# A decoder layer in fp32 quality on one core: batch 1's queries multiplied from raw weights beside batch 0's, and another order of cutting the weights

## What is computed

```
x = layernorm(x + attention(x))        # 16 heads of 64, rope on q and k, causal, w_q w_k w_v w_out
x = layernorm(x + conv(x, context))    # 3 taps, weighed with cosines of neighbouring context columns
x = layernorm(x + ffn(x))              # activations in 8 bits, ternary weights, silu(gate) * up, down
```

## Time and profile before

| | us |
|---|---|
| median of 3 runs | 1465.19 (1463.82 to 1466.19) |
| profiled execution: time, span | 1463.32, 1461.4 |
| set-up, up to the last raw product | 73.2 of the span |
| turn 0 | 73.2 to 142.44 |
| turn 1 | 142.44 to 192.11 |
| PE busy over the span | 1382.8 (95%) |
| DVE, ACT, POOL busy | 1068.1, 613.3, 231.6 |

### The profile page before, as it was taken

One profiled execution on the slowest core, in us unless ns is written; L12 is line 12 of the kernel. 1 busy time (PEld: TensorE's weight loads), 2 busy tenths in 40 slices (PEclk: granted clock), 3 DMA queues, 4 the chain that ended last, 5 costly groups with the idle time before them and its releaser, 6 DMA issues.

```text
span 1461.4 us, 23278 instructions
## 1 busy us (share of the span) xinstructions
PE 1382.8 (95%) x7576; PEld 695.5 (48%) x7576; DVE 1068.1 (73%) x1846; ACT 613.3 (42%) x1203; POOL 231.6 (16%) x270
## 2 busy tenths in 40 slices
PE   6787999999989999999999969999999999999996
PEld 2343555555545555554554544444444444444443
DVE  2886554555477787777877577888888888888884
ACT  4765654555455455445545342222222222222221
POOL 0112121212112221321322311000000000000000
PEclk9898999999999999999999979999999999999999
DMA  9502635454434534444443177222222222222200
GB/s 367 211 14 103 208 128 176 130 191 140 157 118 140 176 117 163 144 143 157 141 172 116 49 250 180 85 74 72 75 83 72 72 72 72 72 72 72 72 19 24
DMA packets 63570, 178.91 MB, mean 122 GB/s; under 512 B 15360, under 2 KB 26672, under 8 KB 63536
## 3 DMA queue, kind: packets, MB, share of 16 engines
q1 hardware_dynamic: 63536, 178.48, 37.5%
HBM read 153.02 MB, written 25.43 MB: 122 GB/s over the span
## 4 chain that ended last, share of the span: by engine, by line
PE 44%; issue 42%; DVE 5%; POOL 3%; ACT 2%; DMA 2%; SPq 1%; POOLq 0%; ACTq 0%; DVEq 0%
PE ps L484 36%; PE ps L475 3%; PE ps L576 2%; PE ps L558 2%; DMA ctx<-ctx 1%; POOL q L1324 1%; ACT tern L831 1%; DVE weights L1024 1%; PE ps L533 1%; ACT prob L753 1%; POOL rstd L1319 1%; DVE weights L1023 1%; DVE negmax L1058 0%; DVE prob L1069 0%; SPq L363 0%
## 5 line engine op out<-in xcount | busy, mean ns | idle before, releaser
L484 PE MATMUL ps<-weights,xT 128*128 128x512 f16 x2160 | 484.6, 381 | 0.0
L484 PEld LDWEIGHTS ps<-weights,xT 128*128 128x128 f16 x2160 | 209.7, 98 | 242.4 <-issue 9.8
L629 PE MATMUL ps<-weights 128*128 128x512 fp8e4 (+1 forms) x1536 | 300.0, 357 | 0.9 <-issue 0.9
L629 PEld LDWEIGHTS ps<-weights 128*128 128x128 bf16 x1536 | 146.7, 98 | 156.0 <-issue 1.4
L484 PE MATMUL ps<-weights 128*128 128x512 f16 x768 | 171.6, 384 | 7.6 <-issue 6.2
L851 ACT ACTIVATE weights<-ps,xscale 128x512 f32<-128x512 f32 x96 | 61.7, 643 | 249.2 <-PE ps L629 249.2
L655 PE MATMUL ps<-weights 128*128 128x512 fp8e4 x704 | 157.3, 380 | 0.0
L753 ACT ACTIVATE prob<-prob,negmax,undo 128x128 f32<-128x128 f32 x256 | 122.7, 482 | 20.7 <-DVE negmax L1060 20.7
L484 PEld LDWEIGHTS ps<-weights 128*128 128x128 f16 x768 | 75.7, 99 | 100.5 <-issue 10.7
L655 PEld LDWEIGHTS ps<-weights 128*128 128x128 bf16 x704 | 67.7, 98 | 76.0 <-issue 0.5
L1319 POOL TENSOR_TENSOR rstd<-rstd,expo 128x1 f32<-128x1 f32 x32 | 17.3, 541 | 535.9 <-DVE rstd L953 535.9
(11 more groups left out here) (145 smaller groups left out, 1836.9 us busy)
## 6 DMA issues: line engine op xcount, KB each, us to landing
wch<-w_ffn SPq DMA_DIRECT2D x96, 688.0 KB, 4.3
wch<-sim_scratch SPq DMA_DIRECT2D x96, 128.0 KB
ternary_scratch<-tern SPq DMA_DIRECT2D x48, 172.0 KB, 1.9
ctx<-ctx SPq DMA_DIRECT2D x16, 512.0 KB
weights<-x SPq DMA_DIRECT2D x16, 512.0 KB, 10.5
x_scratch<-weights SPq DMA_DIRECT2D x16, 512.0 KB, 2.9
weights<-x_scratch SPq DMA_DIRECT2D x16, 512.0 KB, 3.3
out<-k SPq DMA_DIRECT2D x16, 512.0 KB, 2.7
```

Of the source, the lines that this page charges most:

```text
L484: ins = nc.tensor.matmul(ps[:, bank], partsT[:, a, t], weights[:, t, w, half * HALF:(half + 1) * HALF], start=(t == 0 and a + w == 0), sto ...
L629: ins = nc.tensor.matmul(ps[:, 2 * w + a, 0:n], xqT[:, t], w8m[:, t, at:at + n], start=(t == 0), stop=(t == KT - 1))
```

## The change

Batch 1's queries (j = 0 and 2) are multiplied in `first_qkv(0)` too, in fp32 from the same raw tiles of w_q, into the two banks `OB` that the attention's output uses later; `proj(0)` and `proj(2)` of turn 0 fall away. The input of batch 1 is loaded right after that of batch 0 and ahead of all weights. ACT squares w_q and w_k without a break, then makes batch 1's high part, squares w_v, makes the high parts of w_k, squares w_o. The four norms come earlier on PE and alternate between banks 4 and 5. ACT makes the high parts of tiles 8 to 15 and 20 to 31. Turn 0 has an order of its own on PE, ACT, DVE and POOL: all eight absolute sums stand at its end on ACT, the context's sums behind the cuts on DVE. Later turns are as before (their code moves into `turn_rest`, not shown). The diff, cut to its core; the two waits added in `scores` and `pv` hold back writes to banks 4, 6 and 7 until `w_factors(3)` and the ropes of batch 1's queries have read them.

```diff
-SPLITS_ACT = [n for n in range(4 * KT) if n % 4 and not 2 * KT <= n < 3 * KT]
...
-                if t == KT - 1:
+                if t == KT - 1 and m == 0:
+                    eng.wait_ge(q1_full, 2)
+                elif t == KT - 1:
                     eng.wait_ge(pj_full[1], m + 1)
                 else:
                     eng.wait_ge(raw_used, (KT - 1) * m + t + 1)
...
-        NORM = 7
+        NORM = 4
...
                     sp.dma_start(weights[:, n + 2:n + 4] if n < 4 * KT - 2 else wo_raw[:], w.rearrange("(k p) n -> p k n", p=P)[:, 2 * h:2 * h + 2]) \
                         .then_inc(w_in[m][h], 16)
-                if m == 0:
-                    sp.dma_start(x_in[:], xT_in[1]).then_inc(x_loaded, 16)
...
                 if has_next2:
                     sp.wait_ge(parts_ready, b + 2)
+                    if isinstance(b, int) and b == 0:
+                        sp.wait_ge(q1_full, 2)
...
                 m, half = ((0, 0), (1, 0), (0, 1), (1, 1), (2, 0), (2, 1))[j]
-                if j == 0:
+                if isinstance(n, int) and n == 1:
+                    if j in (0, 2):
+                        return
+                    pe.wait_ge(parts_ready, 2)
+                    pe.wait_ge(w_split, (m + 1) * KT)
+                elif j == 0:
...
                 pe.wait_ge(w_squared, KT * (m + 1))
-                nc.tensor.matmul(ps[:, NORM, KT * m:KT * (m + 1)], ones, wsq[:, m], start=True, stop=True) \
-                    .then_inc(w_norm, 1)
+                if m >= 2:
+                    pe.wait_ge(w_norm_sum, m - 1)
+                nc.tensor.matmul(ps[:, NORM + m % 2, 0:KT], ones, wsq[:, m], start=True, stop=True).then_inc(w_norm, 1)
...
                 at = (PJ, TR, PJ)[m]
+                if m == 0:
+                    pe.wait_ge(x_loaded, 16)
...
                         pe.wait_ge(w_in[m][t // 2], 16)
-                    for half in range(2):
-                        ins = nc.tensor.matmul(ps[:, at + half], v[:, t * P:(t + 1) * P],
-                                               weights[:, KT * m + t + 2, half * HALF:(half + 1) * HALF],
-                                               start=(t == 0), stop=(t == KT - 1))
-                        if t == KT - 1:
-                            ins.then_inc(pj_full[half], 1)
+                    for xb, bank in ((v, at), (x_in, OB)) if m == 0 else ((v, at),):
+                        for half in range(2):
+                            ins = nc.tensor.matmul(ps[:, bank + half], xb[:, t * P:(t + 1) * P],
+                                                   weights[:, KT * m + t + 2, half * HALF:(half + 1) * HALF],
+                                                   start=(t == 0), stop=(t == KT - 1))
+                            if t == KT - 1 and bank == OB:
+                                ins.then_inc(q1_full, 1)
+                            elif t == KT - 1:
+                                ins.then_inc(pj_full[half], 3 if m == 2 and half == 0 else 1)
                     if t < KT - 1:
                         ins.then_inc(raw_used, 1)
-                    if t == (KT - 1, KT - 2, KT - 3)[m]:
-                        w_total(m)
...
+                    if isinstance(b, int) and b == 0:
+                        pe.wait_ge(w_norm_sum, 4)
...
+                    if isinstance(b, int) and b == 0:
+                        pe.wait_ge(q1_free, u + 1)
...
+                if isinstance(b, int) and b == 0:
+                    qk_T(0)
+                    proj(1)
+                    scores(0)
+                    qk_T(1)
+                    proj(3)
+                    scores(1)
+                    prob_T(0)
+                    proj(4)
+                    pv(0)
+                    prob_T(1)
+                    pv(1)
+                    proj(5)
+                    for c in range(2):
+                        pe.wait_ge(pj_free[c], pj_out(b))
+                        pe.wait_ge(oT_ready, b * 2 + 2)
+                        product(PJ + c, oT, w_parts[:, 3], c, 3 * KT if c == 0 else None).then_inc(pj_full[c], 1)
+                    return
...
+                def turn_first():
+                    for w in range(2):
+                        copy_bank(w, tr_pair(0, 0), qkT[:, w])
+                    for n in range(2 * KT + 5, 3 * KT):
+                        high_w(n)
+                    act.wait_ge(scores_full, 1)
+                    for w in range(2):
+                        copy_bank(w, tr_pair(0, 1), qkT[:, w])
+                    exps(0)
+                    high_w(3 * KT)
+                    high_w(3 * KT + 1)
+                    for w in range(2):
+                        copy_bank(w, tr_pair(0, 2), probT[:, w])
+                    exps(1)
+                    high_w(3 * KT + 2)
+                    high_w(3 * KT + 3)
+                    oT_high_part(0)
+                    act.wait_ge(pv_full, 1)
+                    for w in range(2):
+                        copy_bank(w, tr_pair(0, 3), probT[:, w])
+                    high_w(3 * KT + 4)
+                    oT_high_part(1)
+                    v_chunk(1, 0)
+                    for n in range(3 * KT + 5, 4 * KT):
+                        high_w(n)
+                    act.wait_ge(ctx_loaded, 32)
+                    nc.scalar.square(sq[:], ctx9[:]).then_inc(ctx_squared, 1)
+                    abs_chunk(0)
+                    v_chunk(1, 1)
+                    abs_chunk(1)
+                    high_x(2)
+                    for c in range(2, SUMS):
+                        abs_chunk(c)
+                if first:
+                    turn_first()
+                    return
...
-            for n in range(KT):
+            for n in range(2 * KT):
                 square(n)
-                if n == 1:
-                    high_x(1)
-            for n in range(2 * KT):
-                square(n + KT)
-                if n in SPLITS_ACT:
-                    high_w(n)
+            high_x(1)
+            for n in range(2 * KT, 3 * KT):
+                square(n)
+            for n in range(KT, 2 * KT):
+                high_w(n)
+            for n in range(3 * KT, 4 * KT):
+                square(n)
...
-                dve.wait_ge(pj_full[j % 2], pj_uses(n, j) + 1)
+                raw = isinstance(n, int) and n == 1 and j in (0, 2)
+                if raw:
+                    dve.wait_ge(q1_full, j // 2 + 1)
+                else:
...
                 dve.wait_ge(roped, n * 4 + j)
-                src = ps[:, PJ + j % 2]
+                src = ps[:, OB + j // 2 if raw else PJ + j % 2]
+                factor = scale0[:, 3:4] if raw else FOLD
...
+                def turn_first():
+                    rope(1, 0)
+                    split_w(2, range(4, 6))
+                    rope(1, 1)
+                    mask_max(0)
+                    split_w(2, range(6, KT))
+                    normalise(0)
+                    mask_max(1)
+                    rope(1, 2)
+                    split_w(3, range(1))
+                    rope(1, 3)
+                    normalise(1)
+                    split_w(3, range(1, 3))
+                    oT_low_part(0)
+                    split_w(3, range(3, 4))
+                    x_maximum(2)
+                    oT_low_part(1)
+                    split_w(3, range(4, KT))
+                    x_factors(2)
+                    x_undo(2)
+                    ctx_norms()
+                    low_x(2)
+                    ctx_dots()
+                    dve.wait_ge(xres_loaded, 16)
...
+            st.wait(st.done(nc.vector.reciprocal(scale0[:, 3:4], xfit[:, 5:6])))
+            w_factors(0)
+            st.wait(st.done(nc.vector.tensor_tensor(scale0[:, 3:4], wnorm[:, 0, 2:3], scale0[:, 3:4], ALU.mult)))
+            split_w(0, range(5))
+            w_factors(1)
             low_x(1)
-            w_factors(0)
+            split_w(0, range(5, KT))
             first_rope(0)
             first_rope(1)
-            split_w(0, range(KT))
-            w_factors(1)
+            split_w(1, range(3))
+            w_factors(2)
+            split_w(1, range(3, KT))
             first_rope(2)
-            split_w(1, range(2))
             first_rope(3)
-            split_w(1, range(2, KT))
             st.wait(st.done(nc.vector.scalar_tensor_tensor(out=wboth[:, 0:1], in0=wnorm[:, 0, 3:4], scalar=HD ** -0.5,
                                                            in1=wnorm[:, 1, 3:4], op0=ALU.mult, op1=ALU.mult)))
             st.wait(st.done(nc.vector.scalar_tensor_tensor(out=undo[:, 0, 0:1], in0=xfit[:, 7:8], scalar=xfit[:, 7:8],
                                                            in1=wboth[:, 0:1], op0=ALU.mult, op1=ALU.mult)))
-            w_factors(2)
-            split_w(2, range(6))
+            split_w(2, range(4))
+            w_factors(3)
+            st.wait(st.done(nc.vector.tensor_tensor(wboth[:, 1:2], wnorm[:, 2, 3:4], wnorm[:, 3, 3:4], ALU.mult)))
+            x_undo(1)
```

(22 more changed lines are left out.)

172 lines of the change are left out of this document (80 added, 92 removed).

## The result

Four runs of the changed kernel have their median at 1457.86 us (1457.05 to 1458.12), four of the kernel before at 1465.69 (1463.82 to 1468.58): 7.8 us less, ratio 0.9944 with the 95% interval 0.9931 to 0.9956. That is faster by more than the 0.2% that can be told from no change. The profiled execution has a span of 1455.1 us (time 1457.05).

A forecast was written before the change was run, and what follows sets the result against it. The start was taken as bound by VectorE's late chain with holes. Turn 1's scores 11.3 us earlier, less 1.7 for clock, gave 9.6 off 1465.19: 1455.6 us; own range 1451.5 to 1459.5 (chance 0.66), whole range 1450 to 1461.

The forecast's parts named there:

- TensorE's part: Raw products at the start: 13.7 us of added fp32 products nearly paid for by vanishing stops, ending at 74.5 instead of 73.2.
- VectorE's chain: First norm to last wo cut: starts 23.8 instead of 29.66, 82.2 busy plus 7.8 holes and 2.2 gaps, ends 116.0.
- the two tight places: Turn 0: first fp16 product 76.0 to 81.8, wanted by VectorE at 82.5; last v product and second probabilities' work ending 114.8.
- The additions: Turn 0: five overlaps of VectorE low parts with GpSimd rope additions, priced at +0.85 us each, 4.3 together.
- The rival built on it: Turn 0: GpSimd additions block whole low parts, up to 1.7 us each, S 4.2 later, 1459.8 us; chance 0.10.
- The sums: End of turn 0: eight absolute sums on ScalarE end at 136.1, delaying turn 1's scores to 137.3, 11.3 us earlier than before.
- S: End of ScalarE's last high part of wo in turn 0, forecast at 113.9; the context square and all eight sums follow.
- The clock: Turn 1: TensorE's stop before the scores costs 1.7 us through a lower clock, a term between 0 and 1.7.
- Later turns, the second phase and the DMA volume are unchanged: 0.: After turn 1: nothing further gained or lost, 0 us.
- The gain is not whole: Rival at turn 1's start: the sums keep up, only TensorE sets it, whole 17.1 us gained, 1448.1; chance 0.10.
- The raw work is hidden: Rival at the start: TensorE's 13.7 us lie on the path at full price, scores 12.6 later, 1468.2; chance 0.08.
- The pace of tiles: Rival in turn 0: eleven tiles at the old 2.2 us instead of 1.3, 9.9 us more, 1465.5, no change; chance 0.06.

The follow-up runs named there:

- copies_sooner: Changed kernel with ScalarE's first two copies of turn 1 moved ahead of the last two absolute sums of turn 0; 1454.73 us, ratio 0.9922 to the kernel before.
- input_late: Changed kernel with batch 1's input loaded behind wq again, as before the change; 1463.02 us, ratio 0.9993 to the kernel before.
- four_products_more: Changed kernel with four unused fp32 products (3.4 us) added ahead of the norm of wo; 1457.00 us, ratio 0.9943 to the kernel before.
- queries_in_fp16: Changed kernel with batch 1's queries again fp16 products in turn 0, and norm products re-placed; 1464.07 us, ratio 0.9988 to the kernel before.
- context_sooner: Changed kernel with turn 1's first copies ahead of the last two sums and its context loads ahead of the next FFN chunks; 1451.06 us, ratio 0.9904.
- second_look: The changed kernel unaltered, run again for a second profile; 1457.02 us, ratio 0.9949 to the kernel before.
- all_three_b: Changed kernel with first copies of turn 1, its context loads and the norm product of wq all moved earlier; 1448.64 us, ratio 0.9881.

## Why the prediction held

*Forecast 1455.6, measured 1457.86: 2.3 us above, inside the likeliest case's own range (1451.5 to 1459.5).* The gain is 7.8 instead of 9.6; the other 0.5 is that the kernel before has its median at 1465.69 now and not at 1465.19.

*A reading that was wrong.* The last stop of turn 0 in the kernel before, 6.24 us ahead of the output product, does not end with VectorE's last cut (129.49): the product takes its tiles one by one, and its first is long cut. Of ScalarE's timeline of before:
```profile
127.25 1.33 ACT L730 ACTIVATE wch<-wch 128x1376 f32<-128x1376 f32 x1
...
128.58 1.33 ACT L730 ACTIVATE wch<-wch 128x1376 f32<-128x1376 f32 x1
...
129.91 0.57 ACT L691 ACTIVATE v<-ps 128x512 f32<-128x512 f32 x1
```
The copy of v out of the bank that the product needs ends at 130.48, and the product begins at 130.58. The copy stands behind two absolute sums, and they behind the last high parts, which wait for VectorE. So the sums were on the path in the old kernel too. The forecast does not use this reading: it goes by the scores of turn 1.

*TensorE's part.* Right in each step: norm products at 23.43 and 33.95 with no wait (23.2 and 33.9 forecast), wq done at 41.04 (41.15), a stop of 3.46 (3.7), raw products' end at 74.84 (74.5). One term was off: the first product began at 11.36, not 10.35; only about 1.75 us, not 2.6, went to half clock behind it, so the norm was on time by luck: two errors of about 1 us cancelled. The first product's start scatters from 10.6 to 12.7.

*VectorE's chain.* Forecast 92.2 long, measured 92.68. Of the parts, the busy time was 81.0 (80.54 of the window, and 0.5 outside it) instead of 82.2. The holes and gaps are 11.6 instead of 10.0: 9.7 that have a releaser, with two that I had not listed: VectorE waits 1.24 for a q addition and 0.66 for a second high half of the output. Of the two tight places the first held (first fp16 product 76.68 to 82.0, no wait of VectorE). The second did not: the last v product ended 2.3 later than forecast, at 117.06, after stops of 5.14 and 1.96 us. It cost nothing, because TensorE was ready for turn 1's scores at 133.64 (131.5 forecast) and the copies came later still; its stop there was 4.22 instead of 5.8.

*The additions.* I priced five overlaps at +0.85, 4.3 together. Four show on VectorE, about 1.0 each: 4.68 for three low parts (two together take 2.48 where nothing disturbs them, so three some 3.7), 3.49 for 2.48, 1.26 for a single-column operation that takes 0.22 elsewhere, and 1.77 for 0.69. With the 1.24 of the new wait that is 5.3, 1 us more than the 4.3. The times of the rows fit taking turns: the addition at 49.44 begins within the first low part and takes 2.24 instead of 1.27, the next low part then stands until it ends at 51.68. The operation at 66.77 ends with the addition, at 68.03, and nothing of it overlaps. This is what the Trainium skill says (SBUF — State Buffer, Who interferes with whom), and the runs agree. The rival built on it priced each meeting at 1.7, from the longest addition; it is 1.0. The additions of 1.7 us in the kernel before begin while VectorE is in another part (at 36.17, where a high part runs from 36.01 to 36.75), so their length holds a wait of their own.

*The sums.* S was forecast at 113.9 and measured at 115.12; from there the last sum ended 21.7 later (22.2 forecast), and the scores started at 137.86 (137.3). The shift is 10.73 instead of 11.3. copies_sooner and input_late show both ends of this link.

*The clock.* 1.7 forecast; in turn 1 TensorE's busy time is 51.23 instead of 49.67, 1.56 more. From the scores of turn 1 to turn 2 it is 43.52 us before and 45.01 and 46.49 in the two profiles after, so the term is 1.5 to 3.0. The length of the stop does not give its price: 4.22 us cost 1.5 and 4.78 us cost 3.0, while 6.24 us in the kernel before cost 1.5. That fits the Trainium skill (TensorE: Matmul & The Clock Gate, What's actually happening), by which the clock is watched in a free-running manner. But where I took the whole 1.7 for the upper end, one of the two went beyond it.

*The step that was mis-sized* is the last: "Later turns, the second phase and the DMA volume are unchanged: 0." In the profiled execution it is 0.6 in turn 2 (50.31 instead of 49.68) and 2.3 in turn 15. The 2.3 are not there in every kernel that has the change (four_products_more), but they enter the time when they fall. The two profiled executions differ by 6.3 us and the medians by 7.8, so the medians hold less of them than this one pair; how much is not known, since executions without a profile have no turn 15 to look at.

*The rivals.* The gain is not whole, and the sums are why: with two of them behind the copies TensorE has no stop before the scores (copies_sooner). The raw work is hidden: queries_in_fp16 ends its raw products 6.4 us sooner (68.4 against 74.8) and starts turn 1's scores 8.3 later, and four more products leave the time as it is. The pace of tiles did not fall back to that of before: VectorE's last low parts follow each other at 1.2 to 1.3 us (pairs in 2.47 and 2.48), not at 2.2.

## What to carry to other kernels

Where an engine stands early in a kernel, look for work that it will have to do later on the same data and that no one has to prepare: here 13.7 us of slower products cost nothing that shows, and 10.5 us of faster ones left a place where another engine would have waited for them. When a chain gets shorter, work out at once which queue stands next at the same point: eight sums in one row took 4.2 us of it back, and moving only the first waiting instruction ahead of the last two (copies_sooner) moved the stop to the next dependent, the exponents, in its profile. And look with a profile at the stop that an experiment was to take away: context_sooner had a lower median, but the stop that it was made for was in neither profile.

## What the runs showed of the hardware

- A VectorE operation on one column took 1.26 us instead of 0.22 (one of the same shape elsewhere) when it began 0.02 us after a GpSimd addition of 128x512 began; a low part of 1.28 us that began 0.16 before the addition kept its length, and the addition took 2.24 instead of 1.27. Whoever is first runs; the other waits it out.
- A chain of some 120 VectorE instructions that depend on four other engines took 92.68 or 92.69 us in four profiles of three kernels (after, second_look, context_sooner, input_late) whose starts lie up to 7 us apart. In the four others with the same order it took 92.81 to 94.56, longer where TensorE came late for VectorE (0.44 and 1.66 us in four_products_more and all_three_b).
- The first weight tile, of the same order of loads, was there between 10.6 and 12.7 us in eight profiles.
